# A two-layer conditional kernel on one core: A rows of both first tiles gathered ahead of both B rows, and the splits of the first pair put in another order

## The chip, the cores and the metric

The kernel runs on one core of one Trainium2 chip. The number that counts is the device time of one execution in microseconds (us), from the device's own timer; lower is better. The engines work side by side and wait for each other only by semaphores: PE is TensorE (matmuls), ACT is ScalarE, DVE is VectorE, POOL is GpSimd, SP is SyncE, which here only issues transfers. Every engine takes its own instructions strictly in the order written. Transfers of SP and gathers of POOL share the core's 16 DMA engines.

## The reference, cut to what matters

`x` has 64 sequences of 32 rows and 512 features. Each sequence names one of 16 low-rank adapters (first index) and one of 16 mixing matrices (second index).

```python
def lora_add(base, inp, A, B):               # rank 16, one adapter per sequence
    t = einsum('bri,bni->bnr', A[0][idx], inp)
    return base + einsum('bor,bnr->bno', B[0][idx], t) * 0.5

gate = lora_add(einsum('bnh,fh->bnf', x, W_gate), x, A_gate, B_gate)     # F = 1376
up   = lora_add(einsum('bnh,fh->bnf', x, W_up), x, A_up, B_up)
act  = silu(gate) * up
x = x + lora_add(einsum('bnf,hf->bnh', act, W_down), act, A_down, B_down)
x = x + einsum('bct,bcd->bdt', x, weights[idx2])                          # 32 x 32 mix
```

## The kernel before, in words

Every float32 operand of a matmul is held as a high part (ACT rounds it, `hi`, line 515) and a low part (DVE subtracts, `lo`, line 805), and each product is three matmuls: high times high (line 1225), high times low (1226), low times high (1227). So an array is usable on PE only after it has landed, ACT has made its high part and DVE its low part. This work is called the split of that array.

A tile is 128 rows, four sequences; two tiles make a pair, and eight pairs pass through gate and up. The feature axis is cut into three sections, `s` = 0, 1, 2, of 352, 512 and 512 columns, so a pair has six units (section, tile) 0 to 5. For each unit PE does `base` (gate, then up, 12 matmuls each) and `lora` (4 matmuls, lines 1292 and 1293), which adds the adapters. The second half of the program is the down projection (line 1393) with the mix.

What `lora` needs of a tile in the first pair comes in this chain:

- POOL gathers the A rows of the tile, one gather for each of its four sequences (`gather_first_a`), and the B rows of a section with one gather (`gather_b`). One gather is one DMA_INDIRECT of line 455. POOL starts them after `rows_ready` and one more wait.
- `split_a` on ACT and DVE puts A beside the gate weights. PE multiplies x by A (`t_alone`, 12 matmuls of 128 columns), which gives t.
- DVE masks t (line 900) and turns it (905), ACT and DVE split it (`split_t`, tiles `tT_hi`, `tT_lo`).
- `split_b` on ACT and DVE (line 809) makes `b_gu` of the B rows. `b_raw` and `b_gu` are single for each tile, so the gather of the next section waits until the last `split_b` of that tile is done.

PE's order at the start is: `base` of units 0, 1, 2, then `t_alone(0)`, the gate half of `base` 3, `t_alone(1)`, `lora(0,0)`, the up half of `base` 3, `lora(0,1)`, `lora(0,2)`, `base` 4, `lora(0,3)`, `base` 5 and so on. `base` 4 waits for `gate(0,1)` (unit 1 has left its bank). The last weight pieces of the first pair, 16 to 23 (section 2), are read first by `base` 4; of them 16 and 17 are `t3_gate`, 18 and 19 `b22_gate`, 20 to 23 the same two for up.

Meanwhile SP has queued, in this order: x of tile 0 and the first weight pieces, x of tile 1 (signals `xT_landed[1]`), the other 16 weight pieces of 256 KB, and then x and A of the next pair. ACT and DVE follow the orders written out by hand that the diff changes.

The waits and calls of POOL that set the start (lines 492 to 499):

```python
            pool.wait_ge(rows_ready, 1)
            pool.wait_ge(xT_ready[0], 1)
            gather_first_a(0)
            gather_b(0, 0, 0)
            gather_first_a(1)
            gather_b(0, 0, 1)
```

Of the kernel before, what the change touches and what calls it, by code (L numbers as in the profile page):

```python
# [19 lines left out]
KH = H // P  # L20
# [40 lines left out]
def build(nc, x, xT, w_gate, w_up, w_down, a_gu_rows, a_dn_rows, b_rows0, b_rows1, b_rows2, b_dn_rows, mix_rows,  # L61
# [4 lines left out]
    with ExitStack() as ctx:  # L66
# [93 lines left out]
        xT_landed = by_tile("xT_landed")  # L160
# [21 lines left out]
        xT_ready = by_tile("xT_ready")  # L182
# [269 lines left out]
        @block.gpsimd  # L452
        def _(pool):
            def gather(dst, src, tile, col):
                return pool.indirect_dma_start(  # L455
                    dst, None, src, bass.IndirectOffsetOnAxis(ap=rows[:, tile, col:col + 1], axis=0))

            def gather_first_a(t):
                for q in range(TILE_SEQS):
                    gather(a_raw[t][:, q, :], a_gu_rows, t, q).then_inc(a_first_landed[t], 16)  # L460

            def gather_b(pr, s, t):
                n = SECTIONS[s][1]
                reached(pool, b_ready[t], NS * pr + s)
                gather(b_raw[t][:, 0:2 * n], b_gu_rows[s], 2 * pr + t, TILE_SEQS).then_inc(b_landed[t], 16)

            def gather_a_dn(m, q0=0, q1=TILE_SEQS):
                reached(pool, a_dn_ready, m - 1)
                for q in range(q0, q1):
                    gather(a_dn_raw[m % 2][:, q, :], a_dn_rows, m, TILE_SEQS + 1 + q).then_inc(a_dn_landed[m % 2], 16)  # L470

            def pair(pr):
                for s in range(1, NS):
                    for t in range(2):
                        gather_b(pr, s, t)
                        if pr == PAIRS - 1 and s == 1:
                            gather_a_dn(1, 2 * t, 2 * t + 2)
                if pr + 1 < PAIRS:
                    for t in range(2):
                        gather_b(pr + 1, 0, t)  # L480
                        if pr + 1 == PAIRS - 1:
                            gather_a_dn(0, 2 * t, 2 * t + 2)

            def gather_b_dn(m):
                reached(pool, b_dn_ready, m - 1)
                gather(b_dn_raw[m % 2][:, :], b_dn_rows, m, 2 * TILE_SEQS + 1).then_inc(b_dn_landed[m % 2], 16)

            def gather_mix(m):
                reached(pool, mix_ready, m - 1)
                gather(mix_raw[m % 2][:, :], mix_rows, m, 2 * TILE_SEQS + 2).then_inc(mix_landed[m % 2], 16)  # L490

            pool.wait_ge(rows_ready, 1)
            pool.wait_ge(xT_ready[0], 1)
            gather_first_a(0)
            gather_b(0, 0, 0)
            gather_first_a(1)
            gather_b(0, 0, 1)
            for pr in range(PAIRS):
                pair(pr)
            gather_mix(0)  # L500
            pool.wait_ge(s_used, FAST)
            gather_b_dn(0)
            for m in range(2, TILES):
                gather_a_dn(m)
                pool.wait_ge(down_done, m - 1)
                gather_b_dn(m - 1)
                gather_mix(m - 1)
            gather_b_dn(TILES - 1)
            gather_mix(TILES - 1)
# [3 lines left out]
        def _(sc):  # L513
# [8 lines left out]
            def split_a(pr, t):  # L522
                if pr == 0:
                    sc.wait_ge(a_first_landed[t], 16 * TILE_SEQS)
                else:
                    sc.wait_ge(a_landed[t], 16 * TILE_SEQS * pr)
                reached(sc, t_done[t], pr)
                hi(a_part("hi", t), a_raw[t][:, :, :].rearrange("p q (k c) -> p q k c", k=KH))\
                    .then_inc(a_hi_ready[t], 1)
# [7 lines left out]
            def split_weights(n0, n1):  # L537
                for n in range(n0, n1):
                    sc.wait_ge(gu_landed[n], 16)
                    hi(piece_part(n, "hi"), landed_at(n)).then_inc(w_hi_ready, 1)  # L540
# [146 lines left out]
            split_x(0, 1)  # L687
            split_weights(2 * KH, 4 * KH)
            split_a(0, 0)
            split_weights(4 * KH, 4 * KH + 2)  # L690
            split_b(0, 0, 0)
            split_weights(4 * KH + 2, 5 * KH)
            split_a(0, 1)
            split_t(0, 0)
            split_b(0, 0, 1)
            silu(0, 0)
            split_b(0, 1, 0)
            split_t(0, 1)
            silu(0, 1)
            split_weights(5 * KH, 6 * KH)  # L700
            split_b(0, 1, 1)
            split_a(1, 0)
            silu(0, 2)
# [99 lines left out]
        def _(ve):  # L803
# [248 lines left out]
            split_x(0, 1)  # L1052
            split_weights(2 * KH, 4 * KH)
            split_a(0, 0)
            split_weights(4 * KH, 4 * KH + 2)
            ve.wait_ge(low_landed, 16)
            split_b(0, 0, 0)
            split_weights(4 * KH + 2, 5 * KH)
            split_a(0, 1)
            mask_t(0, 0)  # L1060
            split_t(0, 0)
            mask_t(0, 1)
            split_b(0, 0, 1)
            split_t(0, 1)
            gate(0, 0)
            split_b(0, 1, 0)
            gate(0, 1)
            turn(0, 0)
            turn(0, 1)
            split_weights(5 * KH, 6 * KH)  # L1070
# [509 lines left out]
```

## Time and profile before

| what | value |
|---|---|
| median of 3 runs | 449.8 us (449.45 to 450.18) |
| the profiled execution's own time | 449.22 us |
| its span in the profile | 447.4 us |
| PE busy | 439.1 us, 98% of the span |
| DVE, ACT, POOL busy | 335.8, 212.5, 170.3 us |
| chain that ended last | PE 93%, DMA 2%, POOL 2%, issue 1%, DVE 1% |
| mean clock granted to TensorE | 0.996 of full |

Times in the profile count from the start of the span. In a timeline a row gives the start, the duration, the engine and line, the operation, the tiles written and read, and in brackets how long the engine had been idle before and what released it. Buffer numbers are left out of tile names, so `a_raw` is that of tile 0 or of tile 1, and `b_raw`, `b_gu` likewise; the order tells which. The profile calls `t3` and `b22` weights `t_gate` and `b_gate`, and the columns of A lie in `w_gate`. The span is a little shorter than the time of the execution, which also counts what lies around it.

### The profile page before, as it was taken

To read this page: it belongs to the slowest core of one execution; us is meant where nothing else is said; L and a number is where in the kernel's file an instruction comes from. 1 tells how busy PE (TensorE), PEld (TensorE's weight loads), DVE (VectorE), ACT (ScalarE), POOL (GpSimd) and SP (SyncE) were. 2 spreads that over 40 slices of the span, in tenths; PEclk is the share of its full clock that TensorE was granted. 3 is DMA by queue.
4 is the path that set the end of the run, shared out by engine and by line. 5 is a ranking of instruction groups with operands and counts; after the bars stand their busy time and mean duration, and the time that the engine had idled before them with its cause. 6 is when DMAs were issued, how large, how long until landed. Compare 5 with 4: busy or idle time off the path is not lost.

```text
span 447.4 us, 7255 instructions
## 1 busy us (share of the span) xinstructions
PE 439.1 (98%) x2477; PEld 394.7 (88%) x2477; DVE 335.8 (75%) x625; ACT 212.5 (47%) x397; POOL 170.3 (38%) x156
## 2 busy tenths in 40 slices
PE   7989999999999999999999999999999999999997
PEld 5868888888888888888888888999999999999996
DVE  6858989888866867867857858977767766776665
ACT  6736345456444444444543444844444454444541
POOL 2711322130111221121121452675666766666630
PEclk9989999999999999999999999999999999999999
DMA  8965664448476565565565599847667666656631
GB/s 240 379 209 159 167 174 134 111 163 199 120 197 158 146 180 149 159 172 146 158 171 145 144 283 347 241 136 194 210 186 209 208 197 179 175 174 191 195 100 47
DMA packets 99987, 81.12 MB, mean 181 GB/s; under 512 B 50960, under 2 KB 83344, under 8 KB 99952
## 3 DMA queue, kind: packets, MB, share of 16 engines
q1 hardware_dynamic: 88512, 47.15, 37.9%
q0 software_dynamic: 11008, 33.30, 24.8%
q8 instruction: 19, 0.31, 0.3%
q10 hardware_dynamic: 432, 0.22, 0.2%
q14 instruction: 16, 0.13, 0.1%
HBM read 65.18 MB, written 15.47 MB: 180 GB/s over the span
## 4 chain that ended last, share of the span: by engine, by line
PE 93%; DMA 2%; POOL 2%; issue 1%; DVE 1%; ACT 0%; SPq 0%; POOLq 0%
PE bank L1393 28%; PE bank L1271 9%; PE bank L1272 9%; PE bank L1270 9%; PE bank L1225 7%; PE bank L1226 7%; PE bank L1227 7%; PE bank L1292 5%; PE bank L1293 4%; PE bank L1423 2%; POOL a_raw L455 2%; PE bank L1403 2%; DMA a_raw<-in_a_gu_rows,rows 1%; DMA gu_landing<-in_w_gate 1%; PE bank L1408 1%
## 5 line engine op out<-in xcount | busy, mean ns | idle before, releaser
L455 POOL DMA_INDIRECT b_raw<-in_b_rows,rows x48 | 51.9, 1082 | 189.8 <-DVE b_gu L809 188.4
L1393 PE MATMUL bank<-wd,actT_hi 128*128 128x288 f32 (+1 forms) x636 | 110.1, 295 | 0.1
L1393 PEld LDWEIGHTS bank<-wd,actT_hi 128*128 128x128 f32 (+1 forms) x636 | 93.8, 188 | 2.1 <-issue 0.9
L455 POOL DMA_INDIRECT a_dn_raw<-in_a_dn_rows,rows x64 | 77.7, 1214 | 19.5 <-issue 19.5
L809 DVE SCALAR_TENSOR_TENSOR b_gu<-b_raw,low_rows,b_gu 128x1024 fp32r<-128x1024 f32 (+1 forms) x48 | 55.6, 1158 | 24.2 <-ACT b_gu L515 20.4
L1393 PE MATMUL bank<-wd,actT_lo 128*128 128x288 f32 (+1 forms) x318 | 68.2, 296 | 0.7 <-issue 0.7
L1393 PEld LDWEIGHTS bank<-wd,actT_lo 128*128 128x128 f32 (+1 forms) x318 | 51.0, 188 | 0.4 <-issue 0.4
L515 ACT ACTIVATE b_gu<-b_raw 128x1024 fp32r<-128x1024 f32 (+1 forms) x48 | 46.2, 963 | 9.6 <-DMA b_raw<-in_b_rows,rows 7.8
L605 ACT ACTIVATE act<-bank 128x512 f32<-128x512 f32 (+1 forms) x48 | 26.2, 547 | 44.0 <-PE bank L1293 43.9
L916 DVE TENSOR_TENSOR act<-act,bank 128x512 f32<-128x512 f32 (+1 forms) x48 | 29.9, 623 | 9.2 <-PE bank L1293 7.6
L1292 PE MATMUL bank<-b_gu,tT_hi 128*128 128x512 f32 (+1 forms) x96 | 35.6, 371 | 0.3 <-DVE tT_lo L805 0.3
L805 DVE TENSOR_TENSOR actT_lo<-actT_raw,actT_hi 128x1280 fp32r<-128x1280 f32 (+1 forms) x32 | 27.0, 886 | 11.6 <-issue 7.6
L1293 PE MATMUL bank<-b_gu,tT_lo 128*128 128x512 f32 (+1 forms) x96 | 35.6, 371 | 0.0
L924 DVE STREAM_TRANSPOSE staging<-act 128x512 f32<-128x512 f32 (+1 forms) x48 | 31.3, 653 | 3.7 <-DVE act L916 0.5
L515 ACT ACTIVATE tdT_hi<-tdT_raw 128x128 fp32r<-128x128 f32 x16 | 5.0, 311 | 59.0 <-DVE tdT_raw L1114 55.0
L1225 PE MATMUL bank<-w_gate_hi,xT_hi 128*128 128x480 f32 (+2 forms) x72 | 26.6, 369 | 3.0 <-DVE w_gate_lo L805 2.3
L455 POOL DMA_INDIRECT b_dn_raw<-in_b_dn_rows,rows x16 | 15.9, 991 | 34.6 <-PE bank L1393 23.7
L1226 PE MATMUL bank<-w_gate_lo,xT_hi 128*128 128x480 f32 (+2 forms) x72 | 26.0, 362 | 0.0
L1227 PE MATMUL bank<-w_gate_hi,xT_lo 128*128 128x480 f32 (+2 forms) x72 | 26.0, 361 | 0.0
L515 ACT ACTIVATE actT_hi<-actT_raw 128x1280 fp32r<-128x1280 f32 (+1 forms) x32 | 23.3, 775 | 0.0
L515 ACT ACTIVATE h_hi<-x_sb 128x224 fp32r<-128x224 f32 (+1 forms) x30 | 11.1, 415 | 22.9 <-DVE x_sb L1129 16.6
L1292 PEld LDWEIGHTS bank<-b_gu,tT_hi 128*128 128x128 f32 x96 | 18.2, 189 | 3.1 <-issue 0.4
(180 smaller groups left out, 1009.7 us busy)
## 6 DMA issues: line engine op xcount, KB each, us to landing
actT_raw<-actT_dram SPq DMA_DIRECT2D x16, 640.0 KB
actT_dram<-staging SPq DMA_DIRECT2D x64, 128.0 KB
x_sb<-in_x SPq DMA_DIRECT2D x16, 256.0 KB
xT_raw<-in_xT SPq DMA_DIRECT2D x15, 256.0 KB
out<-out_sb SPq DMA_DIRECT2D x15, 256.0 KB
a_raw<-in_a_gu_rows SPq DMA_DIRECT2D x56, 64.0 KB
actT_dram<-staging SPq DMA_DIRECT2D x32, 88.0 KB
wd_raw<-in_w_down SPq DMA_DIRECT2D x10, 256.0 KB, 5.8
```

Source lines behind the costliest of these rows:

```text
L455: return pool.indirect_dma_start(dst, None, src, bass.IndirectOffsetOnAxis(ap=rows[:, tile, col:col + 1], axis=0))
L515: return nc.scalar.activation(dst, src, ACT.Copy)
L809: return nc.vector.scalar_tensor_tensor(b, raw, low_rows[:, :], b.bitcast(F32), ALU.mult, ALU.subtract)
L1225: pe.matmul(out_, x_hi, hi, start=(first and k == 0), stop=False)
L1226: pe.matmul(out_, x_hi, lo, start=False, stop=False)
L1227: last = pe.matmul(out_, x_lo, hi, start=False, stop=(stops and k == KH - 1))
L1270: pe.matmul(out_, xs[0], hi, start=(first and j == 0), stop=False, skip_group_check=True)
L1271: pe.matmul(out_, xs[0], lo, start=False, stop=False, skip_group_check=True)
L1272: last = pe.matmul(out_, xs[1], hi, start=False, stop=(j == 1), skip_group_check=True)
L1292: pe.matmul(out_, tT_hi[t][:, g, :], b, start=False, stop=False, skip_group_check=True)
L1293: pe.matmul(out_, tT_lo[t][:, g, :], b, start=False, stop=True, skip_group_check=True)\
L1393: last = pe.matmul(ps_down[e][half][:, 0:HALF], a[e][0:n, c, :], wd[0:n, c, part, at:at + HALF], start=(c == 0 and i == 0), stop=(c == NC ...
```

## The change

Three lists are written in another order, and one wait is another.

- POOL: the wait before the first gather is for x of tile 1 to have landed (`xT_landed[1]`), not for x of tile 0 to be split (`xT_ready[0]`). The four A gathers of tile 1 stand ahead of the B gather of tile 0.
- ACT and DVE: `split_a(0,1)` follows `split_a(0,0)` directly. The splits of weight pieces 16 to 19, which stood between them and before the mask of t, come later: 16 and 17 after `split_b(0,0,1)`, 18 and 19 after `silu(0,1)` on ACT and `gate(0,1)` on DVE. `split_b(0,0,1)` stands ahead of the mask and the turn of tile 1.

SP's queue and PE's list are not touched.

```diff
--- before.py
+++ after.py
@@ -490,10 +490,10 @@
                 gather(mix_raw[m % 2][:, :], mix_rows, m, 2 * TILE_SEQS + 2).then_inc(mix_landed[m % 2], 16)
 
             pool.wait_ge(rows_ready, 1)
-            pool.wait_ge(xT_ready[0], 1)
+            pool.wait_ge(xT_landed[1], 16)
             gather_first_a(0)
+            gather_first_a(1)
             gather_b(0, 0, 0)
-            gather_first_a(1)
             gather_b(0, 0, 1)
             for pr in range(PAIRS):
                 pair(pr)
@@ -687,17 +687,16 @@
             split_x(0, 1)
             split_weights(2 * KH, 4 * KH)
             split_a(0, 0)
-            split_weights(4 * KH, 4 * KH + 2)
+            split_a(0, 1)
             split_b(0, 0, 0)
-            split_weights(4 * KH + 2, 5 * KH)
-            split_a(0, 1)
             split_t(0, 0)
             split_b(0, 0, 1)
+            split_weights(4 * KH, 4 * KH + 2)
+            split_t(0, 1)
             silu(0, 0)
             split_b(0, 1, 0)
-            split_t(0, 1)
             silu(0, 1)
-            split_weights(5 * KH, 6 * KH)
+            split_weights(4 * KH + 2, 6 * KH)
             split_b(0, 1, 1)
             split_a(1, 0)
             silu(0, 2)
@@ -1052,19 +1051,19 @@
             split_x(0, 1)
             split_weights(2 * KH, 4 * KH)
             split_a(0, 0)
-            split_weights(4 * KH, 4 * KH + 2)
+            split_a(0, 1)
             ve.wait_ge(low_landed, 16)
             split_b(0, 0, 0)
-            split_weights(4 * KH + 2, 5 * KH)
-            split_a(0, 1)
             mask_t(0, 0)
             split_t(0, 0)
+            split_b(0, 0, 1)
+            split_weights(4 * KH, 4 * KH + 2)
             mask_t(0, 1)
-            split_b(0, 0, 1)
             split_t(0, 1)
             gate(0, 0)
             split_b(0, 1, 0)
             gate(0, 1)
+            split_weights(4 * KH + 2, 5 * KH)
             turn(0, 0)
             turn(0, 1)
             split_weights(5 * KH, 6 * KH)
```

On POOL, at the start of the program, the rows before (`a_raw0` and `b_raw0` belong to tile 0; `in_b_rows0` is section 0):

```order
L455 DMA a_raw0<-in_a_gu_rows,rows 128x128 x4
L455 DMA b_raw0<-in_b_rows0,rows 128x704
L455 DMA a_raw1<-in_a_gu_rows,rows 128x128 x4
L455 DMA b_raw1<-in_b_rows0,rows 128x704
L455 DMA b_raw0<-in_b_rows1,rows 128x1024
```

and now:

```order
L455 DMA a_raw0<-in_a_gu_rows,rows 128x128 x4
L455 DMA a_raw1<-in_a_gu_rows,rows 128x128 x4
L455 DMA b_raw0<-in_b_rows0,rows 128x704
L455 DMA b_raw1<-in_b_rows0,rows 128x704
L455 DMA b_raw0<-in_b_rows1,rows 128x1024
```

The gather of `b_raw0` for section 0 has moved from fifth place to ninth, and those of `a_raw1` have moved up by one.

On DVE, from the split of A of tile 0 in the first pair (`w_gate_lo<-a_raw0`) on, the rows before (the line numbers of the changed file are one lower):

```order
L805 TENSOR_TENSOR w_gate_lo<-a_raw0,w_gate_hi 128x4x4x32
L805 TENSOR_TENSOR t3_gate_lo<-gu_landing,t3_gate_hi 128x512 x2
L809 SCALAR_TENSOR_TENSOR b_gu0<-b_raw0,low_rows,b_gu0 128x704
L805 TENSOR_TENSOR b22_gate_lo<-gu_landing,b22_gate_hi 128x512 x2
L805 TENSOR_TENSOR w_gate_lo<-a_raw1,w_gate_hi 128x4x4x32
L900 TENSOR_TENSOR t_gu<-bank0,mask 128x128 x2
L905 STREAM_TRANSPOSE tT_raw<-t_gu 128x256
L805 TENSOR_TENSOR tT_lo0<-tT_raw,tT_hi0 128x256
L900 TENSOR_TENSOR t_gu<-bank1,mask 128x128 x2
L905 STREAM_TRANSPOSE tT_raw<-t_gu 128x256
L809 SCALAR_TENSOR_TENSOR b_gu1<-b_raw1,low_rows,b_gu1 128x704
L805 TENSOR_TENSOR tT_lo1<-tT_raw,tT_hi1 128x256
```

and now:

```order
L804 TENSOR_TENSOR w_gate_lo<-a_raw0,w_gate_hi 128x4x4x32
L804 TENSOR_TENSOR w_gate_lo<-a_raw1,w_gate_hi 128x4x4x32
L808 SCALAR_TENSOR_TENSOR b_gu0<-b_raw0,low_rows,b_gu0 128x704
L899 TENSOR_TENSOR t_gu<-bank0,mask 128x128 x2
L904 STREAM_TRANSPOSE tT_raw<-t_gu 128x256
L804 TENSOR_TENSOR tT_lo0<-tT_raw,tT_hi0 128x256
L808 SCALAR_TENSOR_TENSOR b_gu1<-b_raw1,low_rows,b_gu1 128x704
L804 TENSOR_TENSOR t3_gate_lo<-gu_landing,t3_gate_hi 128x512 x2
L899 TENSOR_TENSOR t_gu<-bank1,mask 128x128 x2
L904 STREAM_TRANSPOSE tT_raw<-t_gu 128x256
L804 TENSOR_TENSOR tT_lo1<-tT_raw,tT_hi1 128x256
L915 TENSOR_TENSOR act0<-act0,bank3 128x352
```

Four weight splits (`t3_gate`, `b22_gate`) have left the stretch ahead of the split of `a_raw1`. The split of `b_gu0` now stands directly between it and the mask of t, and `b_gu1` and `t3_gate` stand between the split of tile 0's t and the mask of tile 1's.

## Rows read from the trace of the kernel before

**Rows 1.** The page: the span, and its line of busy times by engine.

```profile
span 447.4 us, 7255 instructions
...
PE 439.1 (98%) x2477; PEld 394.7 (88%) x2477; DVE 335.8 (75%) x625; ACT 212.5 (47%) x397; POOL 170.3 (38%) x156
```

**Rows 2.** Timeline of PE: start us, us, instruction, idle before and its releaser.

```profile
21.44 0.22 PE L1225 MATMUL bank<-w_gate_hi,xT_hi 128*128 128x128 f32 x1
...
22.72 0.45 PE L1225 MATMUL bank<-b_gate_hi,xT_hi 128*128 128x512 f32 x1
...
27.28 0.33 PE L1225 MATMUL bank<-w_gate_hi,xT_hi 128*128 128x128 f32 x1 [1.60 <-DVE w_gate_lo L805]
...
29.16 0.51 PE L1292 MATMUL bank<-b_gu,tT_hi 128*128 128x352 f32 x1 [0.33 <-DVE tT_lo L805]
...
34.83 0.39 PE L1292 MATMUL bank<-b_gu,tT_hi 128*128 128x512 f32 x1
...
35.78 0.50 PE L1225 MATMUL bank<-t_gate_hi,xT_hi 128*128 128x512 f32 x1
```

**Rows 3.** Stretches: busy and count by engine, TensorE clock granted, DMA share, GB/s.

```profile
18.00:24.00 6.00, 6.00 (x34) 5.17 (x33) 4.10 (x7) 3.51 (x6) 4.24 (x4) 1.00 1.05 379
24.00:30.00 6.00, 4.07 (x23) 3.34 (x22) 2.81 (x8) 1.74 (x4) 0.00 (x0) 0.94 0.64 226
29.10:32.50 3.40, 3.34 (x10) 2.88 (x11) 2.23 (x6) 1.96 (x4) 0.94 (x1) 0.53 0.18 54
...
40.40:44.80 4.40, 4.40 (x21) 3.62 (x21) 4.33 (x7) 2.07 (x3) 1.15 (x1) 1.00 0.38 119
```

**Rows 4.** Timeline of POOL: its gathers, same columns as the PE timeline.

```profile
8.05 1.08 POOL L455 DMA_INDIRECT a_raw<-in_a_gu_rows,rows  x1 [7.60 <-DVE xT_lo L805]
...
11.98 1.45 POOL L455 DMA_INDIRECT a_raw<-in_a_gu_rows,rows  x1 [0.30 <-issue]
13.73 1.04 POOL L455 DMA_INDIRECT b_raw<-in_b_rows,rows  x1 [0.30 <-issue]
15.08 1.26 POOL L455 DMA_INDIRECT a_raw<-in_a_gu_rows,rows  x1 [0.30 <-issue]
...
19.17 1.28 POOL L455 DMA_INDIRECT a_raw<-in_a_gu_rows,rows  x1 [0.31 <-issue]
20.75 0.94 POOL L455 DMA_INDIRECT b_raw<-in_b_rows,rows  x1 [0.30 <-issue]
...
40.46 1.15 POOL L455 DMA_INDIRECT b_raw<-in_b_rows,rows  x1 [5.15 <-DVE b_gu L809]
```

**Rows 5.** Timeline of ACT: the splits that wait for a landing.

```profile
10.57 0.63 ACT L515 ACTIVATE xT_hi<-xT_raw 128x512 fp32r<-128x512 f32 x1 [0.54 <-DMA xT_raw<-in_xT]
...
18.27 0.64 ACT L515 ACTIVATE w_gate_hi<-a_raw 128x512 fp32r<-128x512 f32 x1 [0.95 <-DMA a_raw<-in_a_gu_rows,rows]
...
20.30 0.79 ACT L515 ACTIVATE b_gu<-b_raw 128x704 fp32r<-128x704 f32 x1 [0.36 <-DMA b_raw<-in_b_rows,rows]
...
25.87 0.63 ACT L515 ACTIVATE w_gate_hi<-a_raw 128x512 fp32r<-128x512 f32 x1 [3.73 <-DMA a_raw<-in_a_gu_rows,rows]
...
44.82 1.06 ACT L515 ACTIVATE b_gu<-b_raw 128x1024 fp32r<-128x1024 f32 x1 [0.74 <-DMA b_raw<-in_b_rows,rows]
```

**Rows 6.** Timeline of DVE: the steps between a landing and TensorE.

```profile
6.74 0.42 DVE L805 TENSOR_TENSOR xT_lo<-xT_raw,xT_hi 128x256 fp32r<-128x256 f32 x1
...
19.55 1.28 DVE L805 TENSOR_TENSOR t_gate_lo<-gu_landing,t_gate_hi 128x512 fp32r<-128x512 f32 x2
21.21 0.95 DVE L809 SCALAR_TENSOR_TENSOR b_gu<-b_raw,low_rows,b_gu 128x704 fp32r<-128x704 f32 x1 [0.38 <-ACT b_gu L515]
...
27.14 0.48 DVE L900 TENSOR_TENSOR t_gu<-bank,mask 128x128 f32<-128x128 f32 x2
...
32.38 0.52 DVE L916 TENSOR_TENSOR act<-act,bank 128x352 f32<-128x352 f32 x1
32.81 1.28 DVE L809 SCALAR_TENSOR_TENSOR b_gu<-b_raw,low_rows,b_gu 128x1024 fp32r<-128x1024 f32 x1
```

## The prediction

> **What bounds the kernel now.** I read the page first: PE is busy 439.1 of 447.4 us [rows 1]. From `base` 4 on, PE's row ends where the next begins, so a delay ahead of that point moves everything behind it, and only a hole in PE can be won. I therefore went through PE's timeline for holes. It has two in the stretch that the change touches [rows 2]: 1.60 us before `t_alone(1)` at 27.28, ended by DVE's low part of A of tile 1, and 0.33 us before `lora(0,0)` at 29.16, ended by `tT_lo`. Third, the stretches: from 29.10 to 32.50 the granted clock is 0.53, the lower of the two levels (1.2 GHz for 2.4), with 10 matmuls in 3.4 us [rows 3]; PE had been idle just before. So the stage loses some 1.9 us in holes and about 1.6 us in the slow stretch. Last I followed the first hole back: DVE waited for ACT, ACT for the landing of the last A gather of tile 1 (ACT starts at 25.87 [rows 5]), and that gather had started on POOL only at 19.17 [rows 4]. Since POOL's gathers follow each other with 0.3 us between them, this hole is set by when POOL starts and by what stands ahead on it. The measure of the stage is the start of `base` 4, 35.78 now.
>
> **POOL's start.** Now POOL's first gather starts at 8.05. DVE's low part of x of tile 0 ends at 6.74 + 0.42 = 7.16 [rows 6], so it takes 0.89 us from the signal. The new wait ends when x of tile 1 has landed. ACT starts on just that at 10.57, after 0.54 us of idleness that its landing ended [rows 5]. POOL should start at 10.5 + 0.9 = 11.4, which is 3.35 us later. The lower bound is 0.3 us after the landing, the gap that POOL otherwise shows [rows 4]: 10.8.
>
> **POOL's order.** Four A gathers and the gap behind them take 13.73 - 8.05 = 5.68 us, the second four 20.75 - 15.08 = 5.67, one B gather 15.08 - 13.73 = 1.35 [rows 4]. So the last A gather of tile 0 starts at 11.98 + 3.35 = 15.3. The last of tile 1 starts at 11.4 + 5.68 + 4.09 = 21.2, where 4.09 is 19.17 - 15.08: the B gather ahead of it is gone (1.35), the start is 3.35 later, and 2.0 us of delay is left. The B gather of tile 0 starts at 11.4 + 11.35 = 22.75 for 13.73, 9.0 us later; that of tile 1 at 24.1 for 20.75.
>
> **From a gather to ACT.** Three rows say how long this takes while weights still land: 18.27 - 11.98 = 6.3, 20.30 - 13.73 = 6.6, 25.87 - 19.17 = 6.7 us [rows 4, 5]. The DMA engines were full from 18 to 24 (share 1.05) and at 0.64 over the next 6 us [rows 3]. Another says how long it takes with the engines at 0.38: 44.82 - 40.46 = 4.4 us [rows 3 to 5]. For the last A gather of tile 0, in the full stretch, I take 6.3. For the last A of tile 1, at 21.2, I take 5.2, and for B of tile 0 at 22.75, 4.9, nearer to the row of the lighter stretch. The reason: gathers that moved before 24 us now move later, so the weights drain earlier, and the B gather of section 1 (now queued right behind, since it waits for `split_b(0,0,0)`) no longer shares the engines. Bounds for both: 4.4 and 6.6.
>
> **PE up to `t_alone(1)`.** ACT starts on A of tile 0 at 15.3 + 6.3 = 21.6. From ACT's start on A of tile 1 to PE's use of it are 27.28 - 25.87 = 1.41 us, so `t_alone(0)` starts at 23.0 for 21.44. This is a new hole of 1.6 us. `t_alone(0)` takes 22.72 - 21.44 = 1.28, the gate half of `base` 3 takes 27.28 - 1.60 - 22.72 = 2.96 [rows 2], so PE arrives at 27.25. A of tile 1 is usable at 21.2 + 5.2 + 1.4 = 27.8, for 27.28 now: putting it ahead of B does not bring it earlier, because the new wait costs more than the overtaking gives.
>
> **`lora(0,0)`.** Now the chain is: mask at 27.14 [rows 6], PE at 29.16, 2.02 us. The mask now stands behind `split_b(0,0,0)`, whose data were long there before, and will be the latest input. ACT starts on B at 22.75 + 4.9 = 27.65. DVE follows 21.21 - 20.30 = 0.91 later [rows 5, 6], takes 0.95 (0.07 less to the next start), the mask begins at 29.45 and `lora(0,0)` at 31.45. That is 2.3 us later than 29.16. At the bounds 4.4 and 6.6 the shift is 1.8 and 4.0; with POOL's early start too, 1.2.
>
> **From there to `base` 4.** Two chains run side by side. On PE: 34.83 - 29.16 = 5.67 to `lora(0,2)` at now's mix of both clock levels, and 35.78 - 34.83 = 0.95 to `base` 4 [rows 2]: 6.62. On DVE, from the end of `tT_lo` of tile 0 (2.02 - 0.14 = 1.88 behind its mask): `split_b(0,0,1)` 0.95, two weight splits 1.28, the same 1.88 for tile 1, `gate(0,0)` 0.52, `split_b(0,1,0)` 1.28 [rows 6]. That is 5.9, and about 0.3 less since each start overlaps the end before it: 5.6, then `lora(0,2)`, 0.95, in all 6.55 behind `lora(0,0)`. So both chains come out level, and `base` 4 starts at 31.45 + 6.6 = 38.05, a shift of 2.3. The B gather of section 1, which used to start early, must now wait for `split_b(0,0,0)`; released at about 29.4, it takes 4.4 and ACT has it at 33.9, before DVE needs it near 36.
>
> **Edits that I cost at nothing.** Pieces 16 and 17 are split before the mask of tile 1, well ahead of `base` 4. Pieces 18 and 19 come behind `gate(0,1)`, which `base` 4 waits for anyway; PE reads piece 18 after six products of 512 columns, 1.4 us, and DVE has both lows 1.28 us after `gate(0,1)`. The cover is thin: without it the cost is 0.2 to 0.6 us. DVE's later work is pushed back by 1.28 us but `base` 4 and 5 last longer than its splits. SP's A loads for the next pair wait for A of the first and start later, with some 10 us to spare.
>
> **Sum.** Profiled execution: 449.22 + 2.3 = 451.5. The median stands 0.6 above that execution, so 452.1.
>
> **What the pages add.** These sentences are not needed for the sum. The Trainium skill, DMA: Bandwidth & Descriptors, Anatomy of one DMA — SWDGE (gpsimd) path, fits one such transfer as about 2.0 us plus its bytes over 436 GB/s. For B of tile 0 (128 rows of 704 floats, 360 KB) that is an estimate of 2.8 us, and the sum by it would be about +0.2 or less; the 6.3 to 6.7 us of the loaded rows and the 4.4 of the light one disagree with it. The rival that it suggests is the second below.
>
> **Rivals.**
> 1. The loaded latency persists: B takes 6.6 us although the weights have drained. For it: three of the four rows. Against it: the engines' share falls to 0.64 after 24. `lora(0,0)` at 33.15, a shift of 4.0: 453.8.
> 2. Not slower: transfers by an emptying queue are faster than any row here. Even at POOL's early start the B gather stands at 22.15, and for `lora(0,0)` at 29.16 ACT would have to start at 25.35, so the landing must take under 3.2 us. Then A of tile 0 is there at 15.3 + 3.2 + 1.4 = 19.9, before PE wants it, and both holes ahead of `lora(0,0)` close. The time is 449.8, at 2.5 us it is 449.1. Against it: the shortest row is 4.4, and DVE's chain still holds `base` 4 at 6.55 behind `lora(0,0)`.
> 3. The clock. The hole is split in three: 1.6, 0.5 and 2.2 us. If the lower level already holds at `lora(0,0)` and for as long again, its four matmuls take 1.18 instead of 0.64 and two of the up products 0.86 instead of 0.46: about +0.8, 452.9. If the level stays full, PE's chain shortens by 1.6 but DVE's of 6.55 stands, and the shift is the same 2.3. The Trainium skill, TensorE: Matmul & The Clock Gate, Part 1: The HAM clock gate, says that the lower level is the default and comes back after idleness; by that rule the longer last hole speaks for a slow stretch again, and the row at 29.10 agrees.
>
> **Chances.** Forecast 0.57, with its own range 451.0 to 453.1; rival 1 0.15; rival 3 0.10; rival 2 0.18, of it 0.10 faster and 0.08 within 0.2%, which is 0.9 us and about what a measurement of this kernel can tell from no change. So faster 0.10, same 0.08, slower 0.82. The range goes from between rival 2 and the forecast to just above rival 1: 449.5 to 454.1.
>
> **What would show it.** POOL's first gather at 11.4, B's of tile 0 at 22.7; ACT's first A split at 21.6; a hole of 1.6 us before `t_alone(0)`; `lora(0,0)` near 31.5 with a hole before it released by `tT_lo`, and in the chain B's landing in place of A's; `base` 4 near 38.1; no new hole behind it. The prediction is wrong if POOL starts near 8 us, if B lands under 3.2 us after its gather starts, or if PE shows holes behind `base` 4.

## The result, and the profile after

The changed kernel takes 451.49 us, the median of 10 runs (451.0 to 452.99), against 449.79 us for 10 runs of the kernel before. The ratio is 1.0048, with a 95% interval of 1.003 to 1.0065: slower by half a per cent, 1.7 us in the medians. On another chip, in the control run below, it was 450.65 against 448.0, a ratio of 1.0068 (1.0041 to 1.0094). The forecast was 452.1, 2.3 us slower.

The profiled execution took 452.99 us. Its page, in answer to [rows 1]:

```profile
span 451.2 us, 7255 instructions
...
PE 441.1 (98%) x2477; PEld 395.8 (88%) x2477; DVE 335.7 (74%) x625; ACT 212.0 (47%) x397; POOL 169.2 (38%) x156
```

POOL's timeline of the changed kernel, in answer to [rows 4]. The first gather starts at 11.73 for 8.05. The last A gather of tile 1 is that at 21.20, and B of tile 0 is the one at 22.45:

```profile
11.73 1.44 POOL L455 DMA_INDIRECT a_raw<-in_a_gu_rows,rows  x1 [11.28 <-DMA xT_raw<-in_xT]
...
16.02 1.02 POOL L455 DMA_INDIRECT a_raw<-in_a_gu_rows,rows  x1 [0.30 <-issue]
...
21.20 0.94 POOL L455 DMA_INDIRECT a_raw<-in_a_gu_rows,rows  x1 [0.30 <-issue]
22.45 1.32 POOL L455 DMA_INDIRECT b_raw<-in_b_rows,rows  x1 [0.30 <-issue]
```

ACT's timeline, in answer to [rows 5]. A of tile 0 arrives at 21.60, A of tile 1 at 24.81 (before: 25.87), B of tile 0 at 27.23 (before: 20.30):

```profile
21.60 0.63 ACT L515 ACTIVATE w_gate_hi<-a_raw 128x512 fp32r<-128x512 f32 x1 [4.74 <-DMA a_raw<-in_a_gu_rows,rows]
24.81 0.63 ACT L515 ACTIVATE w_gate_hi<-a_raw 128x512 fp32r<-128x512 f32 x1 [2.58 <-DMA a_raw<-in_a_gu_rows,rows]
27.23 0.79 ACT L515 ACTIVATE b_gu<-b_raw 128x704 fp32r<-128x704 f32 x1 [1.78 <-DMA b_raw<-in_b_rows,rows]
```

PE's timeline, in answer to [rows 2]. These are `t_alone(0)`, `t_alone(1)`, `lora(0,0)`, `lora(0,2)`, `base` 4, `lora(0,3)` and `base` 5:

```profile
23.01 0.33 PE L1224 MATMUL bank<-w_gate_hi,xT_hi 128*128 128x128 f32 x1 [1.12 <-issue]
...
27.22 0.22 PE L1224 MATMUL bank<-w_gate_hi,xT_hi 128*128 128x128 f32 x1
...
31.02 0.63 PE L1291 MATMUL bank<-b_gu,tT_hi 128*128 128x352 f32 x1 [2.35 <-DVE tT_lo L804]
...
37.88 0.39 PE L1291 MATMUL bank<-b_gu,tT_hi 128*128 128x512 f32 x1
...
38.83 0.50 PE L1224 MATMUL bank<-t_gate_hi,xT_hi 128*128 128x512 f32 x1
...
44.58 0.50 PE L1291 MATMUL bank<-b_gu,tT_hi 128*128 128x512 f32 x1
...
45.77 0.50 PE L1224 MATMUL bank<-t_gate_hi,xT_hi 128*128 128x512 f32 x1
```

The hole of 1.60 us before `t_alone(1)` is gone. In its place stand one of 1.12 us before `t_alone(0)` (1.67 us in the control run below) and one of 2.35 us before `lora(0,0)`, which waits for `tT_lo`. DVE's timeline shows what `tT_lo` waited for: the mask (29.01) directly behind the split of B (28.14), and before that 1.97 us of idleness, ended by ACT's part of B. Behind it stand the split of `b_raw1` and two weight splits, before the mask of tile 1 at 33.20:

```profile
28.14 0.95 DVE L808 SCALAR_TENSOR_TENSOR b_gu<-b_raw,low_rows,b_gu 128x704 fp32r<-128x704 f32 x1 [1.97 <-ACT b_gu L515]
29.01 0.48 DVE L899 TENSOR_TENSOR t_gu<-bank,mask 128x128 f32<-128x128 f32 x2
...
30.45 0.42 DVE L804 TENSOR_TENSOR tT_lo<-tT_raw,tT_hi 128x256 fp32r<-128x256 f32 x1 [0.48 <-ACT tT_hi L515]
31.13 0.95 DVE L808 SCALAR_TENSOR_TENSOR b_gu<-b_raw,low_rows,b_gu 128x704 fp32r<-128x704 f32 x1 [0.26 <-ACT b_gu L515]
32.00 1.29 DVE L804 TENSOR_TENSOR t_gate_lo<-gu_landing,t_gate_hi 128x512 fp32r<-128x512 f32 x2
33.20 0.48 DVE L899 TENSOR_TENSOR t_gu<-bank,mask 128x128 f32<-128x128 f32 x2
...
35.94 1.28 DVE L808 SCALAR_TENSOR_TENSOR b_gu<-b_raw,low_rows,b_gu 128x1024 fp32r<-128x1024 f32 x1 [0.42 <-ACT b_gu L515]
```

The stretches of the changed kernel, in answer to [rows 3] (columns as there; the last three numbers are clock, DMA share and GB/s):

```profile
24.00:30.00 6.00, 4.67 (x30) 4.02 (x28) 2.49 (x5) 1.43 (x2) 1.58 (x2) 1.00 0.61 166
30.00:36.80 6.80, 5.78 (x15) 4.89 (x16) 5.16 (x10) 3.85 (x7) 1.44 (x2) 0.51 0.60 194
```

The lower clock level holds for 6.8 us here, 3.4 us in [rows 3]. `base` 4 starts at 38.83, 3.05 us later than 35.78. This execution is 1.5 us above the median of its kernel, and its long slow stretch goes with that: the two runs of the changed kernel at a mean clock of 0.992 took 452.99 and 452.88, the eight at 0.996 or more 451.0 to 452.15.

### The profile page after: what moved, and what is told of

Its sections match the earlier page's. It is cut to its first block, busy times and chain, and to the rows that moved or that the text cites. A ratio compares the mean times of both kernels' runs of the same rounds, so it can differ in the third digit from the quotient of the medians.

```text
span 451.2 us, 7255 instructions
## 1 busy us (share of the span) xinstructions
PE 441.1 (98%) x2477; PEld 395.8 (88%) x2477; DVE 335.7 (74%) x625; ACT 212.0 (47%) x397; POOL 169.2 (38%) x156
## 4 chain that ended last, share of the span: by engine, by line
PE 92%; DMA 2%; POOL 2%; issue 1%; SPq 1%; DVE 1%; ACT 0%; DVEq 0%; POOLq 0%
PE bank L1392 28%; PE bank L1270 8%; PE bank L1271 8%; PE bank L1269 8%; PE bank L1224 8%; PE bank L1225 7%; PE bank L1226 7%; PE bank L1291 5%; PE bank L1292 4%; PE bank L1422 2%; POOL a_raw L455 2%; PE bank L1402 2%; DMA xT_raw<-in_xT 1%; DMA b_raw<-in_b_rows,rows 1%; PE bank L1407 1%
```

## The experiments

All times are medians, and each ratio is against the kernel before on the same chip. The kernel before took 449.79 us on the chip of the result and 447.5 to 448.0 us on the others, so times of different chips are compared only by their ratios or by their distance from before. The letters W (POOL's wait), G (order of gathers) and S (order of splits) name the three parts of the change. Where rows of a trace are compared, it is one profiled execution of each kernel.

| run | parts | us | before | ratio (95%) |
|---|---|---|---|---|
| changed | W G S | 451.49 | 449.79 | 1.0048 (1.003 to 1.0065) |
| c1_changed_again | W G S | 450.65 | 448.0 | 1.0068 (1.0041 to 1.0094) |
| e1_old_wait | G S | 449.97 | 447.73 | 1.0052 (1.0034 to 1.007) |
| e2_new_wait | W | 447.86 | 447.73 | 1.0006 (0.999 to 1.0022) |
| e3_new_gathers | G | 452.27 | 447.73 | 1.0103 (1.008 to 1.0126) |
| e4_new_splits | S | 450.09 | 448.0 | 1.0051 (1.0033 to 1.0069) |
| e5_filled_hole | W G S, matmuls in the hole | 450.65 | 447.73 | 1.0076 (1.0051 to 1.0102) |
| f1_mask_before_b | W G S, mask of t ahead of B | 450.43 | 448.0 | 1.0059 (1.0038 to 1.008) |
| h1_pieces_back | W G, most of S | 450.29 | 447.5 | 1.0053 (1.0033 to 1.0072) |
| g1_early_lora | own order | 445.99 | 448.0 | 0.9954 (0.9939 to 0.997) |
| g2_early_lora_new_wait | own order, W | 448.74 | 447.5 | 1.0025 (1.0015 to 1.0035) |
| g3_early_lora_no_wait | own order, no wait | 445.79 | 447.5 | 0.997 (0.9957 to 0.9983) |

**e1_old_wait: the wait undone.**

```diff
-            pool.wait_ge(xT_landed[1], 16)
+            pool.wait_ge(xT_ready[0], 1)
```

> The changed kernel with one edit undone: POOL waits again for xT_ready[0]. Theory A (the extra time is POOL's later start, which delays every gather, B of tile 0 most): POOL starts at 8.0, the last A gather of tile 1 at 17.8 and B of tile 0 at 19.4; ACT has B at about 26, lora(0,0) at about 29.8, no hole before t_alone(0), base 4 0.5 to 1.0 us behind that of before. Time 450.2 to 450.8, half or more of the loss gone. Theory B (the reordered splits cost the time): still 451.3 or more, with lora(0,0) near 31.

POOL and ACT of this kernel. The gather of B starts at 18.66, 3.8 us earlier than in the changed kernel, and ACT has B at 26.51, 0.7 us earlier:

```profile
17.32 1.03 POOL L455 DMA_INDIRECT a_raw<-in_a_gu_rows,rows  x1 [0.30 <-issue]
18.66 1.36 POOL L455 DMA_INDIRECT b_raw<-in_b_rows,rows  x1 [0.30 <-issue]
```

```profile
22.94 0.63 ACT L515 ACTIVATE w_gate_hi<-a_raw 128x512 fp32r<-128x512 f32 x1 [4.46 <-DMA a_raw<-in_a_gu_rows,rows]
26.51 0.79 ACT L515 ACTIVATE b_gu<-b_raw 128x704 fp32r<-128x704 f32 x1 [2.94 <-DMA b_raw<-in_b_rows,rows]
```

The ratio stays at 1.0052. Theory A, that the later start is the loss, falls, and the time is that of theory B; `lora(0,0)` starts at 30.31, between the two forecasts, after one hole of 3.48 us. A part of the loss may still be the wait's: `base` 4 starts at 37.60, 0.6 us earlier than in the control c1, and the distance from before is 2.2 us against 2.65, which the intervals do not tell apart. The gather of B took 7.85 us from its start to ACT here, 4.78 in the changed kernel.

**e2_new_wait: the wait alone**, in the kernel before.

```diff
-            pool.wait_ge(xT_ready[0], 1)
+            pool.wait_ge(xT_landed[1], 16)
```

> The kernel before with the new wait alone. Theory A: POOL at 11.7, a hole of 1.5 us before t_alone(0), the last A gather of tile 1 at about 22.8 and its landing near 27, lora(0,0) at 30 to 30.8 released by A of tile 1, time 450.8 to 451.5. Theory B: within 0.2% of before, because the gathers of the drained queue land sooner and make up for the start.

```profile
22.28 1.46 POOL L455 DMA_INDIRECT a_raw<-in_a_gu_rows,rows  x1 [0.30 <-issue]
```

```profile
22.98 0.33 PE L1225 MATMUL bank<-w_gate_hi,xT_hi 128*128 128x128 f32 x1 [1.73 <-DVE w_gate_lo L805]
...
27.78 0.33 PE L1225 MATMUL bank<-w_gate_hi,xT_hi 128*128 128x128 f32 x1 [0.43 <-DVE w_gate_lo L805]
...
29.65 0.40 PE L1292 MATMUL bank<-b_gu,tT_hi 128*128 128x352 f32 x1 [0.32 <-DVE tT_lo L805]
...
35.17 0.39 PE L1225 MATMUL bank<-t_gate_hi,xT_hi 128*128 128x512 f32 x1
```

The last A gather starts at 22.28, 3.1 us later than in [rows 4], and A of tile 1 is there only 0.5 us later: PE begins `t_alone(1)` at 27.78 for 27.28. Some of the one hole has moved ahead of `t_alone(0)`, 1.73 us, and the rest shrank to 0.43. The ratio of 1.0006 cannot be told from no change. The mechanism that I had expected (POOL's start and the hole at `t_alone(0)`) is there and the loss is not. This profile had the full clock throughout the stage, and `base` 4 starts at 35.17. It is the best measure of the old order of splits at a full clock, since the profile of before held a slow stretch; DVE starts `split_b(0,1,0)` at 32.81 in both.

**e3_new_gathers: the order of gathers alone.**

```diff
             gather_first_a(0)
+            gather_first_a(1)
             gather_b(0, 0, 0)
-            gather_first_a(1)
```

> The kernel before with the new order of gathers alone; waits and splits stay. Theory A: on ACT the split of B of tile 0 stands ahead of that of A of tile 1, so A of tile 1 waits for B's landing at 26 although it has landed; lora(0,0) near 31.7, time about 452. Theory B (only the landing of A of tile 1 counts): A earlier by 1.35, time about 449.

```profile
26.84 0.79 ACT L515 ACTIVATE b_gu<-b_raw 128x704 fp32r<-128x704 f32 x1 [7.12 <-DMA b_raw<-in_b_rows,rows]
...
28.58 0.61 ACT L515 ACTIVATE w_gate_hi<-a_raw 128x512 fp32r<-128x512 f32 x1
```

```profile
30.56 0.47 PE L1225 MATMUL bank<-w_gate_hi,xT_hi 128*128 128x128 f32 x1 [4.85 <-DVE w_gate_lo L805]
```

In the old order of splits ACT takes B (26.84) and two weight pieces ahead of A of tile 1 (28.58). PE waits 4.85 us. Theory A had this mechanism but expected about 452 over a kernel before at 449.8, which is 2.2 us; it was 4.5. So the gathers in this order need the new order of splits: behind the old one they cost twice the loss of the whole change. The clock was at its lower level for 6.8 us in the profile, and the mean clock was 0.992 in all six runs.

**e4_new_splits: the order of splits alone.** The two lists of ACT and DVE in the diff of the change, and nothing on POOL; on DVE its core is:

```diff
-            split_weights(4 * KH + 2, 5 * KH)
-            split_a(0, 1)
             mask_t(0, 0)
             split_t(0, 0)
+            split_b(0, 0, 1)
+            split_weights(4 * KH, 4 * KH + 2)
             mask_t(0, 1)
```

> The kernel before with the new order of splits alone; POOL's wait and gathers as before. Theory D (what costs is that DVE's mask of t stands behind split_b(0,0,0)): B has landed long before, but its split now runs between A of tile 1 and the mask, so the mask begins about 1 us later, lora(0,0) at 30 to 30.4, base 4 at 36.6 to 37.4, time +0.2 to +0.35% of before. Rival (the splits' order alone costs nothing): within 0.1%.

DVE and PE of this kernel. ACT takes B at 26.22 without waiting for it (in [rows 5] it is there at 20.30, from a gather that starts no earlier than here), and still its split (27.11) stands between A of tile 1 and the mask (27.98). Then PE waits for DVE three times, at `lora(0,0)`, `lora(0,1)` and `lora(0,2)`:

```profile
27.11 0.95 DVE L808 SCALAR_TENSOR_TENSOR b_gu<-b_raw,low_rows,b_gu 128x704 fp32r<-128x704 f32 x1
27.98 0.48 DVE L899 TENSOR_TENSOR t_gu<-bank,mask 128x128 f32<-128x128 f32 x2
```

```profile
29.99 0.40 PE L1291 MATMUL bank<-b_gu,tT_hi 128*128 128x352 f32 x1 [1.35 <-DVE tT_lo L804]
...
34.20 0.40 PE L1291 MATMUL bank<-b_gu,tT_hi 128*128 128x352 f32 x1 [0.58 <-DVE tT_lo L804]
...
36.27 0.53 PE L1291 MATMUL bank<-b_gu,tT_hi 128*128 128x512 f32 x1 [1.19 <-DVE b_gu L808]
...
37.34 0.40 PE L1224 MATMUL bank<-t_gate_hi,xT_hi 128*128 128x512 f32 x1
```

The loss is 0.51%, where theory D gave it 0.2 to 0.35%, and within the intervals it is that of the whole change. `lora(0,0)` and `base` 4 stand where D had them, but the comparison was with a profile of before that held a slow stretch; here the clock was full throughout, and still `base` 4 is 1.6 us behind [rows 2]. Against e2, where the clock was full too, it is 2.2 us behind (37.34 for 35.17), about the 2.1 us between the medians. Of these, 0.3 us are there at `lora(0,0)` and 1.8 arise behind it: 7.35 us to `base` 4 for 5.52.

**c1_changed_again: the control.** The changed kernel without an edit.

> The changed kernel once more, as the control on the same chip as the others of this call: 0.3 to 0.65% over before by any theory. Theory E (the landing of B of tile 0 is set by when the weights have drained, not by when its gather starts) expects ACT to have B at about 27, as with the old wait (26.5).

```profile
30.89 0.40 PE L1291 MATMUL bank<-b_gu,tT_hi 128*128 128x352 f32 x1 [2.36 <-DVE tT_lo L804]
...
35.10 0.40 PE L1291 MATMUL bank<-b_gu,tT_hi 128*128 128x352 f32 x1 [0.58 <-DVE tT_lo L804]
...
37.17 0.50 PE L1291 MATMUL bank<-b_gu,tT_hi 128*128 128x512 f32 x1 [1.18 <-DVE b_gu L808]
...
38.19 0.39 PE L1224 MATMUL bank<-t_gate_hi,xT_hi 128*128 128x512 f32 x1
```

Its profiled execution had the full clock, and `base` 4 starts at 38.19 all the same: `lora(0,1)` waits 0.58 us for `tT_lo`, `lora(0,2)` 1.18 us for `b_gu`. ACT has B at 27.10, as theory E expected, from a gather that starts at 22.25.

**e5_filled_hole: matmuls in the hole.**

```diff
                 t_alone(1)
+                ones(10)
                 lora(0, 0)
```

> The changed kernel with 10 matmuls of ones between t_alone(1) and lora(0,0), into a bank that the next product starts anew; results are not used. Theory A (the hole brings the lower clock level, and that stretch costs up to 1.7 us or twice that): granted clock 1.0 throughout the stretch from 24 to 38, base 4 at 37.4 to 37.7, held by DVE's chain, time 450.2 to 450.8 against 451.5. Rival C (the clock falls anyway, or DVE's chain holds base 4): no change.

No gain, as rival C said. In the profile the clock fell even earlier (0.51 from 25.2 to 28.6), after the hole before `t_alone(0)`, and `lora(0,2)` at 37.09 still waited for DVE's `b_gu`. The ten matmuls ran from 30.19 to 32.56, so `lora(0,0)` came 1.9 us after the end of `tT_lo` (30.66), where 0.15 us is usual, and `base` 4 at 38.12 did not move: a second sign that DVE's chain holds this point. The kernel is not a clean test of the clock, because the filling came behind the first hole.

**f1_mask_before_b: t of tile 0 ahead of B of tile 0.**

```diff
             split_a(0, 1)
-            split_b(0, 0, 0)
             split_t(0, 0)
+            split_b(0, 0, 0)
```

and the same on DVE, with `mask_t(0, 0)`.

> The changed kernel with one edit more: ACT and DVE mask and split t of tile 0 ahead of the split of B of tile 0. Theory D: mask at 26.2, B is the last input of lora(0,0), which starts at 29.2 to 29.5 instead of 31.0; DVE's chain behind it moves with it, base 4 at 36.5 to 37.2, so 1.2 to 1.8 us are won back of the changed kernel and the time is within 0.15% of before. Rival F (B's landing alone holds the stage, mask order is nothing): no change against the changed kernel.

```profile
30.25 0.38 PE L1291 MATMUL bank<-b_gu,tT_hi 128*128 128x352 f32 x1
...
35.83 0.50 PE L1291 MATMUL bank<-b_gu,tT_hi 128*128 128x512 f32 x1 [1.31 <-DVE b_gu L808]
...
36.88 0.40 PE L1224 MATMUL bank<-t_gate_hi,xT_hi 128*128 128x512 f32 x1
```

`base` 4 comes at 36.88, 1.3 us before that of the control, within the 36.5 to 37.2 expected. The time missed: within 0.15% of before was expected, and it is 0.59% above. The fastest run is 449.06 against 450.21 of the control, but the medians differ by only 0.2 us, within what these intervals can tell. Its runs spread more (up to 452.82 at a mean clock of 0.992). So mask behind B is one part of the loss, shown in the profile and not settled in the time. `lora(0,0)` starts without a hole, later than expected, since a slow stretch (0.52 from 25.2 to 28.6) had held PE's own work ahead of it: `t_alone(1)` starts at 28.97 for 27.09 in the control. The hole of 1.31 us that is left, before `lora(0,2)`, waits for `b_gu` of section 1. Its gather is released only when `split_b(0,0,0)` is done and starts at 29.43, but ACT takes the data at 33.40 without waiting for them, behind `tT_hi` and `silu(0,0)`. So the order on DVE and ACT is what the trace shows there, and not the gather.

**h1_pieces_back: weight pieces 16 and 17 split again behind A of tile 0.**

```diff
             split_a(0, 0)
+            split_weights(4 * KH, 4 * KH + 2)
             split_a(0, 1)
...
             split_b(0, 0, 1)
-            split_weights(4 * KH, 4 * KH + 2)
```

> The changed kernel with weight pieces 16 and 17 split again right behind A of tile 0, on ACT and DVE, where both engines idle; all else as changed. Theory G (behind lora(0,0) DVE's chain holds base 4, and these 1.28 us stand in it): tT_lo of tile 1 near 33.8 for 35.0, lora(0,2) 1.2 us earlier, base 4 near 37.0 where the clock is full, time 0.5 to 1.2 us below the changed kernel, so 0.35 to 0.55% over before. Rival (PE's own chain or the B gather of section 1 holds base 4): no change.

```profile
30.74 0.42 DVE L804 TENSOR_TENSOR tT_lo<-tT_raw,tT_hi 128x256 fp32r<-128x256 f32 x1 [0.48 <-ACT tT_hi L515]
...
33.73 0.42 DVE L804 TENSOR_TENSOR tT_lo<-tT_raw,tT_hi 128x256 fp32r<-128x256 f32 x1 [0.48 <-ACT tT_hi L515]
```

From `tT_lo` of tile 0 to that of tile 1 are now 2.99 us; in the changed kernel 34.64 - 30.45 = 4.19, in e4 4.20. The 1.2 us were in DVE's chain as theory G says, and PE has no hole behind `lora(0,0)`. But the clock was at its lower level from 32.5 to 36.0 in this profile, PE's own chain held `base` 4 at 37.96, and the ratio of 1.0053 lies inside both of the changed kernel's intervals. It is also within the 0.35 to 0.55% expected, but in time the run (6 executions, 448.58 to 450.91) is inconclusive.

**g1_early_lora: a version that beats both.** It starts from the kernel before, gathers and wait untouched. DVE masks t of tile 0 ahead of A of tile 1, where it sat idle for 3.16 us in the trace of before, and `gate(0,0)` goes ahead of the mask of tile 1, with its turn; ACT's list follows. PE does `lora(0,0)` ahead of the up half of `base` 3, and `t_alone(1)` behind the first three products of that half:

```diff
             split_weights(4 * KH + 2, 5 * KH)
-            split_a(0, 1)
             mask_t(0, 0)
             split_t(0, 0)
+            split_a(0, 1)
+            gate(0, 0)
+            turn(0, 0)
             mask_t(0, 1)
             split_b(0, 0, 1)
             split_t(0, 1)
-            gate(0, 0)
             split_b(0, 1, 0)
...
-            base(0, 3, ramp=True, between=ramp_loras)
+            base(0, 3, ramp=True, between=lambda: lora(0, 0), hook=lambda: t_alone(1))
```

> The kernel before, gathers and wait unchanged, reordered by what has landed: DVE masks t of tile 0 in its idle time before A of tile 1, PE does lora(0,0) before the up half of unit 3 and t_alone(1) after that half's first three products, DVE does gate(0,0) before the mask of tile 1. If what limits the stage is the order on DVE and PE around the landing of A of tile 1: no hole before t_alone(1) over 0.3 us, clock full, base 4 at 33 to 34 for 35.8, time 1.8 to 2.7 us under before, 0.4 to 0.6%. Rival: the B gather of section 1 lands last, near 29.4 to 30, and holds lora(0,2), then base 4 at 34.5 and 0.2 to 0.3%.

DVE's row of the kernel before that shows the idle time, and PE of g1 from `t_alone(1)` to `base` 4:

```profile
26.53 0.69 DVE L805 TENSOR_TENSOR w_gate_lo<-a_raw,w_gate_hi 128x512 fp32r<-128x512 f32 x1 [3.16 <-ACT w_gate_hi L515]
```

```profile
27.00 0.33 PE L1227 MATMUL bank<-w_gate_hi,xT_hi 128*128 128x128 f32 x1 [0.16 <-DVE w_gate_lo L805]
...
30.88 0.40 PE L1294 MATMUL bank<-b_gu,tT_hi 128*128 128x352 f32 x1 [0.22 <-DVE tT_lo L805]
...
32.34 0.50 PE L1294 MATMUL bank<-b_gu,tT_hi 128*128 128x512 f32 x1 [0.58 <-DVE b_gu L809]
...
33.38 0.39 PE L1227 MATMUL bank<-t_gate_hi,xT_hi 128*128 128x512 f32 x1
```

The hole before `t_alone(1)` is 0.16 us, and `base` 4 starts at 33.38, 2.4 us before [rows 2]. The time is 0.46% under before. All 12 runs had a mean clock of 0.999 or more, where those of before on this chip had 1.0, 0.996 or 0.992. Against the runs of before at a full clock (447.1) the gain is 1.1 of the 2.0 us; the rest goes with the clock.

**g2_early_lora_new_wait and g3_early_lora_no_wait: the order of g1 with POOL's wait changed.** g2 first, then g3, which waits only for `rows_ready`:

```diff
-            pool.wait_ge(xT_ready[0], 1)
+            pool.wait_ge(xT_landed[1], 16)
```

```diff
-            pool.wait_ge(xT_ready[0], 1)
```

> The reordered kernel (lora(0,0) ahead of the up half, mask of tile 0 in DVE's idle time) with POOL waiting for xT_landed[1]. Theory E (a gather behind the weights lands when they have drained, whenever it starts): A of tile 1 at ACT at 26 to 26.5 for 25.6 although its gather starts 4 us later; but A of tile 0 comes at 21.6, and t_alone(0) waits 1.5 us, so base 4 is 0.5 to 1.2 us behind that of the same kernel with the old wait: time 0.2 to 0.4% below before. If a gather's time is fixed at 6.5 us: A of tile 1 at 28.8 and base 4 at 36, no gain over before.

> The same reordered kernel with POOL waiting for nothing but its row numbers, so its first gather starts at 4.8 to 5.5. Theory E: A of tile 1 lands at 24 to 25.5 though its last gather starts at 15.5, and the early gathers take bandwidth from the first weights: base 0 ends 0.3 to 1 us later; time within 0.15% of the same kernel with the old wait (0.46% below before). If a gather's time is fixed at 6.5 us: A of tile 1 at 22, and a further 0.5 us or more is won.

```profile
23.13 0.33 PE L1227 MATMUL bank<-w_gate_hi,xT_hi 128*128 128x128 f32 x1 [1.26 <-DVE w_gate_lo L805]
...
29.01 0.40 PE L1294 MATMUL bank<-b_gu,tT_hi 128*128 128x352 f32 x1 [1.53 <-DVE tT_lo L805]
```

```profile
11.97 0.43 PE L1226 MATMUL bank<-w_up_hi,xT_hi 128*128 128x352 f32 x1 [0.66 <-DVE w_up_lo L804]
```

g2 missed: 0.2 to 0.4% below before was expected, and it is 0.25% above. `t_alone(0)` has a hole of 1.26 us, `lora(0,0)`, which has none in g1, one of 1.53, and `base` 4 starts at 36.70, 3.3 us behind g1. That is near what was expected of a fixed gather time (`base` 4 at 36), but A of tile 1 is not its cause: ACT took it at 28.32, behind `tT_hi`, so when it landed can't be told. What came late is A of tile 0 (21.72 for 17.75 in g1) and B of tile 0 (24.02, where g1 has it by 20.04), which in g1's order stand ahead of everything. So a late start cost nothing that can be told where A of tile 1 is the last input (e2), about 0.6 us at `base` 4 where B of tile 0 is the last one (c1 against e1), and 3.3 us where A and B of tile 0 come first (g2 against g1). In g3 POOL starts at 4.61 and PE gets a hole of 0.66 us before the last products of `base` 0, whose weights now share the engines with gathers (an inference: the trace shows only that PE waited for `w_up_lo`); nothing is won over g1 (the intervals of 0.997 and 0.9954 overlap). ACT took A of tile 1 at 25.35 without waiting for it, so its landing is not known to be as early as 22.

## Why the prediction was right

The time, its sign and the place are right: 2.3 us were forecast, 1.7 measured in one series and 2.65 in another. The chain of waits in the changed profile goes through B of tile 0, the mask, and `lora(0,0)`, as written. But that the size came out is in good part luck: the chain priced the lateness of B, and the order of splits costs as much when B is early (e4). The steps one by one:

- **POOL's start and order**: 11.4 forecast, 11.73 measured; A of tile 1 last at 21.2 against 21.20; B at 22.75 against 22.45; the last A of tile 0 at 15.3 against 16.02, because the first gather of the run takes 1.44 us.
- **A of tile 0**: ACT at 21.6 against 21.60, `t_alone(0)` at 23.0 against 23.01. Two errors cancel: the gather started 0.7 us later and took 5.6 us for 6.3.
- **A of tile 1**: this step failed. It said that putting A ahead of B does not bring it earlier. ACT had it at 24.81 for a forecast of 26.4, 1.06 us earlier than before, and the hole before `t_alone(1)` closed. From gather start to ACT were 3.6 us; I had taken 5.2, and 4.4 as the lower bound.
- **B of tile 0 and `lora(0,0)`**: 27.65 against 27.23, 31.45 against 31.02. The 4.9 us were 4.78.
- **From `lora(0,0)` to `base` 4**: 6.6 us forecast, 7.30 in c1 with a full clock (30.89 to 38.19) and 7.81 in the profile of the result with the lower level for 6.8 us. DVE's chain was sized 0.7 us short: between its steps it waits 0.26 us for ACT's part of `b_gu` of tile 1 and 0.42 us for that of section 1, which I had left out. That this chain and not PE holds the point at a full clock is shown by c1 and e4, where `lora(0,2)` waits 1.18 and 1.19 us for it, and by e5. The comparison hid this part of the loss: 6.62 us in [rows 2] held a slow stretch, and with the old order of splits at a full clock it is 5.52 (e2). So the new splits cost 1.8 us behind `lora(0,0)`, where the prediction had no loss.
- **No new delay behind `base` 4**: wrong in the profile of the result. From `base` 4 to `base` 5 are 6.94 us for 6.49 in the trace of before. `lora(0,3)` starts at 44.58, just behind DVE's `b_gu` (43.24, 1.28 us long). In c1 it is 6.34 us. The size is that of the thin cover that the prediction named, but the place is not: the `b22_gate` weights come in time (PE reads them from 40.32 without a wait). What failed is the next sentence there, that DVE's later splits, pushed back by 1.28 us, fit under `base` 4 and 5; in this profile DVE had also waited until 38.25 for unit 1, which PE finished late at the lower clock.
- **The new wait as the cause**: wrong. The prediction put the loss on the 3.35 us of later start. W alone costs nothing that can be told (e2), and without W the loss is the same within the intervals (e1). For the two transfers that count, most of the late start is given back: A of tile 1 starts 3.1 us later in e2 than before and comes 0.5 us later, B of tile 0 starts 3.8 us later in the changed kernel than in e1 and comes 0.7 us later. The order of splits alone costs all of it within the intervals (e4, 1.0051): the split of B and later two weight pieces stand in front of the two masks, on an engine that sat idle for 3.16 us in the trace of before. The order of gathers alone is worse still (e3); together with the new splits it adds nothing that these intervals show. At `base` 4 the parts go 35.17 (W alone, full clock), 37.34 (S), 37.60 (G S), 38.19 (W G S, c1), and the distances of the medians from before 0.1, 2.1, 2.2 and 2.65 us: some 0.5 us may be left for W, which only the single profiles show.

Of the rivals, the first (B keeps 6.6 us) did not come true in the changed kernel, though it does in e1 with the early start, at 7.85. The second (under 3.2 us) did not either. The third did in a part of the runs: the lower clock level for twice as long, and the profiled execution was the slowest of its kernel, 452.99 for the rival's 452.9 (whose terms, 0.54 and 0.40 us, add up to 0.9 and not 0.8). Long holes alone did not bring it: c1 has holes of 1.67 and 2.36 us at the same places and kept the full clock.

What stays open: how the 1.3 us that f1 wins at `base` 4 and the 1.2 us that h1 wins in DVE's chain add up in time. Both were near the width of the intervals, and the two edits were not tried together. Nor was it tested that what sets the late landings is the draining of the weights. The DMA engines' share stays near or above 1.0 until about 27 us before, 26 in e1, 24 in e2 and 23 in the changed kernel; besides the weights the gathers themselves ran then, and SP's loads of A for the next pair, which are issued from 21.07 on before and from 24.80 on in the changed kernel.

## What to carry to other kernels

Before a transfer is moved in its queue, ask whether it lands while the engines that carry it are full or as they empty. Here the transfers that landed near the end of the full stretch gave back most of a later start. Those in the middle of it did not: B of tile 0 starts 3.45 us later in e2 than before (17.18 for 13.73) and comes 3.6 us later (23.94 for 20.30), and A of tile 0 starts 4.2 us later in the changed kernel than in e1 and comes 3.75 us later (21.60 for 17.85). In a list of an in-order engine, put first what unlocks the next engine with data that is already there, and put what waits for a landing behind it; here t of tile 0 was there at 22.9 before and its mask ran at 27.14. And when a hole is closed, look for the other small piece of work that can stand in it (g1 did this with the adapter products), rather than for a way to make its input earlier.

## What the runs showed of the hardware that I had not expected

- The time from the start of a gather to the engine that waits for it is not a property of the gather. For B of tile 0 (360 KB): 6.57 us from 13.73 (before), 6.76 from 17.18 (e2), 7.85 from 18.66 (e1) and 7.5 from 19.32 (e3), but 4.78 from 22.45 (changed) and 4.85 from 22.25 (c1). For the last A of tile 1 (64 KB): 6.7 from 19.17 (before), 5.6 from 17.32 (e1), 4.1 from 22.28 (e2), 3.6 from 21.20 (changed). The Trainium skill, DMA: Bandwidth & Descriptors, Anatomy of one DMA — SWDGE (gpsimd) path, fits 2.0 us plus bytes over 436 GB/s, an estimate of 2.1 us for the 64 KB and 2.8 for the 360 KB; every row here is above it, by least for the gathers that start at 21.20 or later.
- The mean clock of a run goes in steps. For the kernel before the time goes with it, on the chip of c1: 447.1 us at 0.999 or 1.0 (9 runs), 448.2 at 0.995 or 0.996 (17), 449.7 at 0.992 (4). For the changed kernel only the last step shows, in the series of the result: 451.2 to 451.6 us at 0.999 or 1.0 (3 runs), 451.0 to 452.15 at 0.996 (5), 452.9 and 453.0 at 0.992 (2); where DVE's chain holds `base` 4, one slow stretch of PE costs nothing that can be told. What decides whether the level falls these runs do not show. It fell in the trace of before (holes of 1.60 and 0.33 us) and in that of the changed kernel (1.12 and 2.35), and stayed full in that of c1 (1.67, 2.36, 0.58 and 1.18). In e2 it stayed full in 9 of 12 runs; in g1, with no hole over 0.6 us behind 20 us, in all 12.
